# Joining the mixer stage and the feed-forward stage of an adaLN block into one block of instructions

## Time and profile before

| what | value |
|---|---|
| median of 3 runs | 1635.58 us (1635.34 to 1636.09) |
| the profiled execution: its own time | 1635.6 us |
| its span, first to last instruction | 1633.8 us |
| mean granted TensorE clock | 0.974 |
| PE busy | 1510.4 us, 92% |
| DVE busy | 1206.1 us, 74% |
| ACT busy | 623.8 us, 38% |
| POOL busy | 306.5 us, 19% |

### The profile page before, as it was taken

How to read it: one execution, slowest core, us unless ns; L and a number is a source line. 1 busy time by engine, 2 the same in 40 slices (tenths; PEclk the granted TensorE clock), 3 DMA queues, 4 the chain that set the end, 5 groups by cost and what they waited for, 6 DMA issues and landing times. The chain is left out here.

```text
span 1633.8 us, 23088 instructions
## 1 busy us (share of the span) xinstructions
PE 1510.4 (92%) x8289; PEld 1233.7 (76%) x8289; DVE 1206.1 (74%) x2556; ACT 623.8 (38%) x1208; POOL 306.5 (19%) x344
## 2 busy tenths in 40 slices
PE   4989999999999999999999999766999999999998
PEld 4977877777777777877777777535888888888887
DVE  3688998998998998998999998734454554643632
ACT  3346455555554554554564564311120111211210
POOL 1302311221221221221121121220111111011011
PEclk9789999999999999999999999877999999999999
DMA  7322222222222122122122122126012012021010
GB/s 252 109 94 78 72 85 79 72 85 78 72 84 79 69 88 78 62 94 79 40 90 88 57 79 75 55 77 238 14 65 78 13 65 78 5 74 52 26 52 27
DMA packets 61412, 124.84 MB, mean 76 GB/s; under 512 B 13296, under 2 KB 15984, under 8 KB 56816
## 3 DMA queue, kind: packets, MB, share of 16 engines
q1 hardware_dynamic: 55632, 114.68, 19.9%
q10 hardware_dynamic: 5664, 8.65, 1.5%
HBM read 97.62 MB, written 25.69 MB: 75 GB/s over the span
## 5 line engine op out<-in xcount | busy, mean ns | idle before, releaser
L780 DVE SCALAR_TENSOR_TENSOR xBC<-conv_in,wconv,xBC 128x256 f32<-128x256 f32 x480 | 230.7, 484 | 12.7 <-ACT xBC L577 1.3
L1369 ACT ACTIVATE silu_gate<-bank,sgate 128x512 f32<-128x512 f32 x88 | 60.5, 688 | 383.3 <-PE bank L1488 383.3
L1423 DVE SCALAR_TENSOR_TENSOR hidden<-bank,sup,silu_gate 128x512 f32<-128x512 f32 x88 | 66.0, 750 | 147.7 <-PE bank L1488 147.7
L576 ACT ACTIVATE conv_in<-bank 128x256 f32<-128x256 f32 x160 | 61.4, 384 | 238.9 <-PE bank L1062 238.9
L1147 PEld LDWEIGHTS bank<-X,decay 128*128 128x128 f32 x1024 | 122.4, 194 | 30.5 <-DVE decay L867 18.9
L1488 PE MATMUL bank<-ff_h_high,W_gate 128*128 128x512 f32 x352 | 141.5, 402 | 2.4 <-DVE ff_h_low L1411 2.4
L1147 PE MATMUL bank<-X,decay 128*128 128x64 f32 x1024 | 125.6, 276 | 16.3 <-DVE X_D L909 16.3
L1488 PE MATMUL bank<-ff_h_low,W_gate 128*128 128x512 f32 x352 | 140.1, 398 | 0.0
L1520 PE MATMUL bank<-W_down,hidden_high 128*128 128x512 f32 x352 | 139.5, 396 | 0.0
L1520 PE MATMUL bank<-W_down,hidden_low 128*128 128x512 f32 x352 | 139.5, 396 | 0.0
L1488 PE MATMUL bank<-ff_h_high,W_up 128*128 128x512 f32 x352 | 139.5, 396 | 0.0
(11 more groups left out here) (170 smaller groups left out, 3300.5 us busy)
## 6 DMA issues: line engine op xcount, KB each, us to landing
decay<-sums_scratch SPq DMA_DIRECT2D x32, 1024.0 KB, 4.8
wq_rows<-wqT SPq DMA_DIRECT2D x33, 256.0 KB, 4.3
widened_scratch<-wq_rows SPq DMA_DIRECT2D x33, 256.0 KB, 2.3
x_tile<-x SPq DMA_DIRECT2D x32, 256.0 KB, 3.2
x_resid<-x SPq DMA_DIRECT2D x32, 256.0 KB, 2.8
x_scratch<-x_resid SPq DMA_DIRECT2D x32, 256.0 KB, 2.0
ff_x_tile<-x_scratch SPq DMA_DIRECT2D x32, 256.0 KB, 4.1
ff_x_resid<-x_scratch SPq DMA_DIRECT2D x32, 256.0 KB, 4.7
```

What stands on the lines that cost most here:

```text
L576: nc.scalar.activation(A.raw[:, m, 3:3 + SC], ps[:, 0:SC], ACT.Copy)
L780: nc.vector.scalar_tensor_tensor(A.xc[b][:, m, :], A.raw[:, m, j:j + SC], A.wconv[:, m, j:j + 1], A.xc[b][:, m, :], ALU.mult, ALU.add).the ...
L1369: nc.scalar.activation(B.sg[m % 2][:], gates[m % 2][:], ACT.Silu, scale=T.sgate[:, m:m + 1]) \
L1423: nc.vector.scalar_tensor_tensor(B.hid[m % 2][:], ups[m % 2][:], T.sup[:, m:m + 1], B.sg[m % 2][:], ALU.mult, ALU.mult).then_inc(hid_step, 1)
```

## The change

The two stages become one block. `feed_forward_stage` becomes a class `FeedForward`, whose parts are called inside the mixer's engine programs.

- **Space.** W_gate, W_up and W_down lie where W_in lay, the feed-forward's small tiles over tiles that the drain doesn't need. The first feed-forward turn reads its h from the mixer's `h_high` and `h_low`.
- **Turns.** Feed-forward turns are now 9: two of 256 tokens, then seven of 512. Both stages keep their order of steps within a turn.
- **Turn 15** of the mixer normalises, as every other turn does, the tokens of the next: these are now the first 256 tokens of x1, with the feed-forward's shift and scale. After its W_in products SP issues the ten weight loads on its own queue (before, ACT issued them). The flag is made here, and DVE spreads the gate columns.
- **The 33 chunks** of weights: two turns (6 and 11) take a third chunk, turn 15 and the drain none or one fewer, so that all are stored before the weights are loaded.
- **The drain** on PE, ACT and DVE is written out with the first feed-forward turn's gate and up products between its steps. It no longer makes the last state (`states` of chunk 1, its `decay_X` and `read_state`). It uses single banks: one for all transposes, one for W_out's product.
- **PE's choice of program** now lies ahead of the drain, so that both programs contain drain and feed-forward.
- In the feed-forward part the normalised x overwrites its tile.

The core of the diff, without changes of indentation:

```diff
+        return accs[r % 2] if n != N else state
+        return tps[(r + off) % 2 if n != N else 0]
+    EXTRA = (6, 11)
...
@@ sync, turn(n, b)
+            if n in EXTRA:
+                load_wq(n, -1)
                 if has_next(n):
                     load_x(after(n), 1 - b)
                 if has_before(n):
                     load_resid(u, b, 0)
+            if n in EXTRA:
+                store_wq(n, -1)
...
-                    elif has_own(n):
+                    elif n != N - 1:
                         load_wq(n, 1)
+                    else:
+                        a_wait(sp, a_filled, n, ("z", 3), 1)
+                        sp.wait_ge(wq_out, NWQ * 16)
+                        ff.load_weights(sp)
                     if has_before(n):
                         wait(sp, out_step, u, 2 * NC, 2 * (c + 1))
                         sp.dma_start(rows(x1_d, 1 - b, u, c), A.xr[:]).then_inc(x1_out[c], 16)
...
+            if n == N - 1:
+                t_wait(sp, t_filled, n, ("ln", 1), 1)
+                ff.load_x(sp, 1)
...
@@ gpsimd: in the drain ff.rstd(pool, 1) stands ahead of residual(n, u, b, 0)
@@ scalar
+        def drain():
+            n, u = N, N - 1
+            ff.silu_gate(act, 0, 0)
+            evac_x(n, u, 0)
+            ff.silu_gate(act, 0, 1)
+            ff.silu_gate(act, 0, 2)
+            evac_B(n, u, 0)
+            evac_x(n, u, 1)
+            ff.silu_gate(act, 0, 3)
+            square(u, 0)
+            evac_g(n, u, 0)
+            ff.silu_gate(act, 0, 4)
...
@@ vector
+        def drain():
+            n, u, b = N, N - 1, 0
+            read_yoff(n, u, b, 0, 0)
+            mask_G(u)
+            scores(u, 0, 0)
+            read_yoff(n, u, b, 0, 1)
+            ff.read_rows(dve)
+            scores(u, 0, 1)
+            ff.hidden(dve, 0, 0)
+            read_ydiag(u, 0, 0)
+            scores(u, 1, 0)
+            read_ydiag(u, 0, 1)
+            decay_X(n, u, 0)
+            ff.hidden(dve, 0, 1)
+            gate(n, u, b, 0)
+            ff.hidden(dve, 0, 2)
+            read_state(u, b, 0, 0)
+            read_state(u, b, 0, 1)
+            ff.hidden(dve, 0, 3)
+            low_g(n, u, 0)
+            read_ydiag(u, 1, 0)
+            scores(u, 1, 1)
+            ff.hidden(dve, 0, 4)
+            read_yoff(n, u, b, 1, 0)
+            ff.hidden(dve, 0, 5)
+            ff.stats(dve, 1, 0)
+            read_yoff(n, u, b, 1, 1)
+            ff.stats(dve, 1, 1)
...
@@ tensor
+        def drain(project):
+            n, u, b = N, N - 1, 0
+            y_off(u, b, 0, 0)
+            scores_G(n, u, b)
+            y_off(u, b, 0, 1)
+            wait(pe, split, N, 2 * NC, 2 * NC)
+            project(0, 0)
+            wait(pe, a_emptied, N, A_USES, -2)
+            wait(pe, G_masked, u, 1, 1)
+            ff.rows(pe)
+            transpose_x(n, u, b, 0)
+            project(0, 1)
+            y_diag(n, u, 0, 0)
+            project(0, 2)
+            y_diag(n, u, 0, 1)
+            transpose_B(n, u, b, 0)
+            project(0, 3)
+            states(n, u, 0, 0)
+            project(0, 4)
+            states(n, u, 0, 1)
+            transpose_x(n, u, b, 1)
+            y_diag(n, u, 1, 0)
+            y_off(u, b, 1, 0)
+            project(0, 5)
+            transpose_g(n, u, 0)
+            project_out(n, u, 0)
+            y_off(u, b, 1, 1)
+            y_diag(n, u, 1, 1)
+            project(0, 6)
+            project(0, 7)
+            project(0, 8)
+            transpose_g(n, u, 1)
+            project(0, 9)
+            project_out(n, u, 1)
+            project(0, 10)
...
+    def tensor(self, pe, drain, last_bank_free):
+        pe.wait_ge(self.flag_step, 2)
+        wide = pe.value_load(self.B.flag[0:1, 0:1], min_val=0, max_val=1)
+        with pe.If(wide == 0):
+            self.program(pe, FR, drain, last_bank_free)
+        with pe.Else():
+            self.program(pe, F32, drain, last_bank_free)
...
+        drain(project)
+        self.transpose_ln(pe, 1, range(0, 2))
+        for g in range(len(self.DOWN_GROUPS)):
+            pe.wait_ge(self.down_w_in[g], 16)
+        down(0, 0)
+        self.transpose_ln(pe, 1, range(2, KD))
+        last_bank_free()
+        down(0, 1)
```

More of the change, by code:

```diff
@@ L322, in mixer_stage @@
     Z = DI - ZQ
[L323 to L361, removed]
-            if n == 0:
[L364 to L453, removed]
-                if has_own(n):
[L456 to L470, removed]
@@ new lines, in a_slot, with a_wait, t_slot @@
+    def a_slot(n, key):
+        if n == 0:
+            return [k for k in A_ORDER if k[0] != "out"].index(key), 0
+        order = A_ORDER if n != N else [k for k in A_ORDER if k[0] == "out"]
+        return order.index(key), -2
+    def a_wait(eng, sem_, n, key, back):
+        r, off = a_slot(n, key)
+        wait(eng, sem_, n, A_USES, off + r + back)
+        return accs[r % 2] if n != N else state
+    def t_slot(n, key):
+        if n == -1:
+            return key[1], 0, 0
+        if n == 0:
+            return key[1], 2, 0
+        order = T_ORDER if n != N else [k for k in T_ORDER if k[0] != "ln" and k != ("x", 1, 2)]
+        return order.index(key), -8, n
@@ new lines, in t_wait, with turns, has_own, wq_chunk @@
+    def t_wait(eng, sem_, n, key, back):
+        r, off, m = t_slot(n, key)
+        wait(eng, sem_, m, T_USES, off + r + back)
+        return tps[(r + off) % 2 if n != N else 0]
+    block = ctx.enter_context(nc.Block())
+    def turns(prologue, turn):
+        prologue()
+        for n in range(N):
+            turn(n, n % 2)
+    def has_own(n):
+        return n != N
+    NWQ = T.wq.shape[0] // P
+    EXTRA = (6, 11)
+    assert NWQ == 2 * N + 1
+    def wq_chunk(n, s):
+        return 2 * n + s + sum(n >= e for e in EXTRA)
@@ L548, in _ @@
[L548 to L556 removed]
+                    else:
+                        a_wait(sp, a_filled, n, ("z", 3), 1)
+                        sp.wait_ge(wq_out, NWQ * 16)
+                        ff.load_weights(sp)
+                if has_before(n):
+                    wait(sp, out_step, u, 2 * NC, 2 * (c + 1))
+                    sp.dma_start(rows(x1_d, 1 - b, u, c), A.xr[:]).then_inc(x1_out[c], 16)
+                    if c == 0:
+                        load_resid(u, b, 1)
@@ new lines, in transpose_ln, with product, project_zdt @@
+                mm.then_inc(t_filled, 1)
+        def product(out, pairs, parts):
+            last = len(pairs) * len(parts) - 1
+            i = 0
+            for wp, ap in parts:
+                for lhs, rhs in pairs:
+                    mm = nc.tensor.matmul(out, lhs(wp, ap), rhs(wp, ap), start=(i == 0), stop=(i == last))
+                    i += 1
+            return mm
+        def project_zdt(n, c):
+            if c == 0:
+                wait(pe, split, n, 2 * NC, 2 * NC)
+            ps = a_wait(pe, a_emptied, n, ("zdt", c), -1)
+            s = slice(c * P, (c + 1) * P)
+            mm = product(ps[:, 0:ZQ + H],
+                         [(lambda w, a, k=k: hT[a][:, k, s], lambda w, a, k=k: Win[w][:, k, Z:Z + ZQ + H])
+                          for k in range(KD)], PARTS)
+            mm.then_inc(a_filled, 1)
@@ new lines, in vector @@
+    def vector(self, dve):
+        self.read_down(dve, 0, 0)
+        self.split_h(dve, 1)
+        self.read_down(dve, 0, 1)
+        for t in range(1, self.N):
+            more = t < self.N - 1
+            for m in range(self.KH):
+                self.hidden(dve, t, m)
+                if more and 1 <= m <= self.NC[t + 1]:
+                    self.stats(dve, t + 1, m - 1)
+                    if m == self.NC[t + 1]:
+                        for c in range(self.NC[t + 1]):
+                            self.norm(dve, t + 1, c)
+            if more:
+                self.split_h(dve, t + 1)
+            for c in range(self.NC[t]):
+                self.read_down(dve, t, c)
```

1962 lines of the change are left out of this document (1058 added, 904 removed).

## The result

| | median | range | runs |
|---|---|---|---|
| before | 1635.46 us | 1634.19 to 1636.09 | 4 |
| changed | 1580.51 us | 1577.78 to 1581.73 | 4 |

The account below looks back on a forecast made before the run. PE was taken to bound the kernel, with 86 us of little work between the stages. Start 1038.9 + work 96.2 + stalls 11.3 + clock 1.2 = 1147.6 us, 39.2 us earlier, gave 1596.4 us; range 1587 to 1609 us.

Parts of the forecast that it names:

- Seven equal turns follow in both kernels: Feed-forward after the two 256-token turns: seven 512-token turns of 63.45 us each, the same before and after.
- Where the drain starts: End of mixer turn 15: PE ready at 1036.5 us, flag at 1037.05, PE's drain starting at S = 1038.9 us.
- The branch: Ahead of the drain, PE's register load and choice of program: 1.8 us, between 0 and 6.05 us.
- PE's work, 96.2 us to the first 512-token turn: Drain and two 256-token turns at full clock without stalls: 63.5 us plus 32.7 us from S.
- The stalls, 11.3 us: PE's waits for DVE and ACT in the drain and both 256-token turns, 11.3 us together.
- The clock, 1.2 us: Idle 2.4 us before the drain may lower PE's clock: 1.2 us, with ends 0 and 2.4 us.
- What is hidden: Weight loads to about 1059 us, SP's later transfers, third chunks in turns 6 and 11, new waits: 0 us.
- Rival 2: Drain and 256-token turns: PE hardly waits, branch 0, no low clock, half the stalls; 1587.8 us, chance 0.11.
- Rival 1: Drain: DVE sets the pace, stalls twice as long; 1607.7 us, chance 0.15.
- Rivals 3: Start of the drain: weights come late, PE stands 17.6 us at the first feed-forward product; 1615.2 us, chance 0.04.
- Rival 4: Drain: the clock stays at 1.2 GHz throughout; 1637.5 us, slower by 1.9 us, chance 0.03.
- Rival 5: Drain: the fill doesn't happen, the drain takes its old 54.8 us, products stand behind it; 1610.1 us, chance 0.05.

Follow-up runs that it names:

- a_w32: The changed kernel with a 32-byte unused tile ahead of W_gate and another behind W_down: 1592.81 us, ratio to before 0.9740.
- b_same: The kernel before with 160 unused bytes behind W_down, so weights and split operands start alike modulo 512: 1621.35 us, ratio 0.9913.
- a_nofill: The changed kernel with all eleven products of the first feed-forward turn, their SiLUs and hidden steps behind the drain's steps: 1599.5 us, ratio to before 0.9784.
- a_h128: The changed kernel with 128 unused bytes behind W_down, weights at 192 and split operands at 320 modulo 512: 1591.51 us in one run.
- a_gt128: The changed kernel with 128 unused bytes ahead of gT_high, aligning the gated rows with W_out modulo 512: 1578.24 us, ratio to before 0.9656.

## Why the prediction was wrong, point by point

**"Seven equal turns follow in both kernels": the step that failed.** It took the 63.45 us of a 512-token turn as a property of its matmuls. It is one of their operands' addresses: where the starts of moving and stationary operand are a multiple of 256 bytes apart a turn takes 61.64 us. The new allocation has this distance, the old one had not, and 12.7 us of my error are due to it: the profiled execution's own time, 1579.7 us, lies 16.7 us below the forecast, and the other 3.9 us are in the steps below. a_w32 takes the 12 us from the changed kernel, b_same gives 14.7 to the old one, with eight turns instead of seven. It was luck that the new allocation fell on this distance: a_w32, the same merge without it, took 1592.81 us, inside the range and 3.6 us below the forecast. Nothing in the trace of before showed it, since there all turns had the same pitch; but every new allocation is a part of a change, and I costed this one at nothing without naming a row.

**Where the drain starts.** PE ready at 1036.5 and flag at 1037.05: PE's last product ended at 1036.35 us and the flag came at 1036.69. **The branch:** I took 1.8 us between 0 and 6.05; load and choice take 1.12 us. S was 1037.86 instead of 1038.9, 1.0 us early. The Trainium skill's rule on taken branches (page "Runtime: NRT & Kernel Launch", section "Instruction fetch mechanics") speaks for a wait at a taken branch, by which the prediction put the step near its upper end, 6.05 us. No such wait is in the trace, here with the fast program written first behind the choice; whether its branch is taken the trace does not tell, and a choice that goes the other way was not run.

**PE's work, 96.2 us to the first 512-token turn:** 64.44 + 33.24 = 97.7 us busy, 1.5 us more. **The stalls, 11.3 us:** 8.0 us, in the forecast places. The up product of m = 3 waited 1.25 us (1.4 forecast), m = 4 0.63 (1.0), `states` 0.27 (0.4), the transposes of x 0.78 each (0.9), `transpose_g` of chunk 0 1.42 + 0.74 (2.5), of chunk 1 1.41 (1.6), the second `y_off` 0.39 (0.5). The largest miss is the second 256-token turn: 0.4 us instead of 2.1. **The clock, 1.2 us:** 0; it stayed at 1.00. Together 1.0 - 1.5 + 3.3 + 1.2 = 4.0 us, against 43.1 - 39.2 = 3.9 us.

**What is hidden:** as forecast. The weights had landed by about 1060 us (forecast 1059) and no product waited for them; SP's transfers behind them were late and no wait of PE hung on them; turns 6 and 11 with their third chunk took the usual 62.5 us.

**The rivals.** Rival 2 (PE hardly waits, 1587.8 us) came nearest and was still too slow, as it shared the failed step. Rival 1 (DVE sets the pace) did not happen: no wait of PE for DVE was above 1.42 us. Rivals 3 and 4 had no sign. Rival 5 (no fill) forecast the first 512-token turn at 1161.3 us; a_nofill, which is that kernel, had it at 1163.98. Rival 4's mechanism is real in it: with holes in the drain the mean clock was 0.72, low in part of the drain rather than all of it.

So of the 55.8 us in the spans, 22.8 (1186.78 - 1163.98) are what remains without the fill (weights under the drain, no start of a second stage; it was not taken apart further), 20.3 the fill, and 12.7 the addresses, which were in no line of the diff that I priced.

## What to carry to other kernels

A change that moves tiles has an unwritten part: in long rows of 512-column products compare the pitch (duration of a chain row by its count) before and after, and try a pad that brings stationary and moving operand to the same start modulo 256 bytes; here it was worth 0.9% of the old kernel for one line. Filling a stage that has holes pays twice, once for the holes and once for the clock, and the second may be the larger. When a forecast says that a stretch is the same in both kernels, name what would have to stay the same for it: matmuls, clock, banks and addresses.

## What the runs showed of the hardware

- **Operand distance.** In the feed-forward turns 512-column products of the fast 4-byte type follow each other every 0.2267 us at a distance of 0 modulo 256 bytes and every 0.232 to 0.234 us at 32, 96 and 128, with the clock at 1.00 in all of them. PE loads the next weights while the moving operand streams (PE and PEld overlap), so the two reads of SBUF may meet; this is argued by exclusion, from the idle DVE, ACT and POOL in a_h128, and neither that they meet nor how is shown. By the Trainium skill, page "SBUF — State Buffer", section "SBUF: two separate sides", only the port pair shared by DVE and GpSimd causes contention among engines, and PE never waits on anyone; section "A bandwidth-pool intuition that's wrong" gives PE a second read port of its own for the weights. By both the place of the operands should cost nothing. The measurement decides: it costs 0.006 to 0.008 us a product.
- **What stays open.** In the mixer W_out's products reached the short pitch only in part when aligned (a_gt128: 0.2273 to 0.232 us), so the distance is not all that counts there, and the products of 256 columns gain nothing: in the changed kernel 16 of them take 1.92 us at distance 0

```profile
1111.94 0.28 PE L1738 MATMUL bank<-ff_h_high,W_gate 128*128 128x256 f32 x1
...
1113.86 0.28 PE L1738 MATMUL bank<-ff_h_high,W_gate 128*128 128x256 f32 x1
```

  and 1.90 us at distance 128 in a_nofill

```profile
1099.57 0.28 PE L1738 MATMUL bank<-h_high,W_up 128*128 128x256 f32 x1
...
1101.47 0.28 PE L1738 MATMUL bank<-h_high,W_up 128*128 128x256 f32 x1
```

  Distances 64 and 192 were not tried, nor other types.
- **The clock.** The granted clock was 1.00 in the drain with the fill and 0.72 in the drain without it. What PE did differently is in the windows: idle for 7.7 of 72.1 us against 15.3 of 60.5 us.
